# A fused state-space and expert kernel on one core: GpSimd's gate products spread over earlier slots, the skip factor folded into a weight

## The reference

```python
x = x + s6(layernorm(x))      # selective state space, 256 inner channels, 64 states
x = x + moe(layernorm(x))     # 8 experts, hidden size 256, top 2 of 8 weighted
x = x + s5(layernorm(x))      # diagonal complex state space, 64 states
x = x + moe(layernorm(x))     # the same experts again
```

```python
xs, res = split(x @ Wi + bi);  xs = silu(xs)
h = dA * h + dB * x_t                     # for each of 256 channels x 64 states
y_t = C_t * sum(h, axis=-1)
y = (y + xs * Dp) * silu(res)
z = y @ Wo + bo + residual                # then a layernorm with gamma, beta
```

## Time and profile before

| | |
|---|---|
| median of 3 runs | 1877.04 us (1875.87 to 1879.06) |
| the profiled execution | 1876.52 us, its span 1874.7 us |
| VectorE busy | 1523.8 us, 81% of the span |
| GpSimd busy | 1513.0 us, 81% |
| TensorE busy | 1333.3 us, 71% |
| ScalarE busy | 1291.4 us, 69% |
| mean granted TensorE clock | 0.861 of full speed |

### The profile page before, as it was taken

How to read it: one execution, slowest core, us unless ns; L and a number is a source line. 1 busy time by engine, 2 the same in 40 slices (tenths; PEclk the granted TensorE clock), 3 DMA queues, 4 the chain that set the end, 5 groups by cost and what they waited for, 6 DMA issues and landing times. The chain is left out here.

```text
span 1874.7 us, 19073 instructions
## 1 busy us (share of the span) xinstructions
PE 1333.3 (71%) x5928; PEld 601.0 (32%) x5928; DVE 1523.8 (81%) x2109; ACT 1291.4 (69%) x2285; POOL 1513.0 (81%) x888
## 2 busy tenths in 40 slices
PE   3236458778776877768776878668786777668958
PEld 1001123224332343324331343324332343324535
DVE  3988998888889788897899878988889878896322
ACT  4456668686787778777787778777787768765423
POOL 0899999978998699977998789986999789983312
PEclk8556569879997999979998899979999899979979
DMA  3511411122111310132111401132111221100000
GB/s 92 187 51 70 163 45 51 48 90 95 57 42 57 135 51 29 51 110 91 38 47 49 157 28 56 48 108 78 51 51 48 90 96 51 46 28 1 7 1 6
DMA packets 38749, 121.90 MB, mean 65 GB/s; under 512 B 5876, under 2 KB 21111, under 8 KB 26359
## 3 DMA queue, kind: packets, MB, share of 16 engines
q1 hardware_dynamic: 37062, 120.67, 18.1%
q10 hardware_dynamic: 1584, 0.01, 0.0%
HBM read 109.13 MB, written 11.53 MB: 64 GB/s over the span
## 5 line engine op out<-in xcount | busy, mean ns | idle before, releaser
L1180 DVE TENSOR_TENSOR_SCAN h<-da,w 128x512 f32<-128x512 f32 x1024 | 1191.0, 1207 | 148.9 <-ACT da L768 130.9
L878 POOL TENSOR_TENSOR w<-ur,br 128x1024 f32<-128x1024 f32 x512 | 1192.5, 2358 | 40.4 <-DVE h L1180 27.6
L768 ACT ACTIVATE da<-dr,al 128x511 f32<-128x511 f32 x1024 | 681.6, 687 | 219.5 <-DVE h L1180 216.5
L601 PE MATMUL ys<-h,wsum 128*32 128x512 f32 x2048 | 320.1, 702 | 222.2 <-DVE h L1180 202.8
L533 PE MATMUL bankH<-nT,w 128*128 128x512 f32 x512 | 309.3, 688 | 90.7 <-DVE aq L1118 86.3
L821 POOL TENSOR_TENSOR x<-x,yk 128x512 f32<-128x512 f32 x128 | 162.6, 1270 | 219.3 <-ACT yk L729 219.2
L547 PEld LDWEIGHTS bankY<-w,aq 128*128 128x128 f32 x2048 | 247.0, 192 | 85.4 <-issue 63.3
L533 PE MATMUL bankG<-nT,w 128*128 128x512 f32 x432 | 250.3, 663 | 24.6 <-DVE aq L1118 24.6
L547 PE MATMUL bankY<-w,aq 128*128 128x128 f32 x2048 | 254.3, 278 | 12.4 <-DVE aq L1118 7.9
L729 ACT ACTIVATE yk<-bankY,rt 128x128 f32<-128x128 f32 x512 | 151.2, 362 | 111.2 <-PE bankY L547 98.0
L601 PEld LDWEIGHTS ys<-h,wsum 128*32 128x32 f32 x2048 | 42.9, 114 | 422.2 <-DVE h L1180 388.0
(11 more groups left out here) (181 smaller groups left out, 1124.7 us busy)
## 6 DMA issues: line engine op xcount, KB each, us to landing
br<-b_rows SPq DMA_DIRECT2D x64, 1024.0 KB, 5.1
dr<-d_rows SPq DMA_DIRECT2D x16, 1024.0 KB, 6.9
ur<-u_rows SPq DMA_DIRECT2D x16, 1024.0 KB, 7.4
d_rows<-vh SPq DMA_DIRECT2D x16, 256.0 KB
u_rows<-th SPq DMA_DIRECT2D x16, 256.0 KB
xnew<-in_L_attn_a_x_dram SPq DMA_DIRECT2D x8, 256.0 KB, 5.2
w<-in_L_ffn_W_dram SPq DMA_DIRECT2D x2, 1024.0 KB, 11.1
x<-in_L_attn_a_x_dram SPq DMA_DIRECT2D x8, 256.0 KB, 9.0
```

Source lines behind the costliest of these rows:

```text
L601: ins = nc.tensor.matmul(ys[32 * q:32 * q + 32, :], wsum[:, :], h[:, (DUOS * t.b + 2 * group + q // 2) % H_RING, q % 2, :], start=(n == 0) ...
L768: A(da[duo % D_RING][:, k % 2, 1:L], dr[:, half, q, 1:L], ACT.Exp, scale=nega[:, QUADS * half + q, n:n + 1]).then_inc(decay_ready, 1)
L878: G.tensor_tensor(w[:, turn_duo % W_RING, :, :], ur[:, half, q:q + 2, :], br[:, chunk % B_RING, row:row + 1, :].to_broadcast([128, 2, L]), ...
L1180: V.tensor_tensor_scan(h[:, turn_duo % H_RING, k % 2, :], da[duo % D_RING][:, k % 2, :], w[:, turn_duo % W_RING, k % 2, :], 0.0, ALU.mult, ...
```

## The change

The products move to other slots and ScalarE's part of the skip term goes away. `cg` is now made in slots 30 and 36, `xd` in slots 33 and 39, `resa` in slot 42. `xd` is now xs * sres, without the factor Dp. Instead, ScalarE once multiplies the rows of Wo by Dp into a new tile `wod` (slot 40 of turn 0, two instructions of 128x128), and TensorE multiplies `xd` by `wod` in place of `wo`. The wait that keeps `xd` from being overwritten before z was computed moves from ScalarE to GpSimd.

```diff
-GATES_AT, RES_AT = 44, 54
+GATES_AT, SKIPS_AT, RES_AT, FOLD_AT = (30, 36), (33, 39), 42, 40
...
+                if known(c, 1):
+                    pe.wait_ge(skips_folded, 2)
                 pe.wait_ge(direct_ready, 2 * c + 2)
                 for a in range(TT):
                     for k in range(2):
-                        nc.tensor.matmul(p[:, a * 128:(a + 1) * 128], xd[:, k, a * 128:(a + 1) * 128], wo[:, k, :],
+                        nc.tensor.matmul(p[:, a * 128:(a + 1) * 128], xd[:, k, a * 128:(a + 1) * 128], wod[:, k, :],
...
-            def skips(t):
-
-                b = t.b
-                for half in range(2):
-                    yield GATES_AT + 3 * half
-                    if half == 0 and t.post:
-                        act.wait_ge(filled[BANK["z"]], t.before("z") + 1)
-                    A(xd[:, half, :], xs[:, half, :], ACT.Copy, scale=dps_[:, half:half + 1]).then_inc(skip_ready, 1)
+            def fold_skips():
+
+                yield FOLD_AT
+                act.wait_ge(late_loads, 16 * LATE_LOADS)
+                for k in range(2):
+                    A(wod[:, k, :], wo[:, k, :], ACT.Copy, scale=dps_[:, k:k + 1]).then_inc(skips_folded, 1)
...
-                weave(pair, [skips(t)] + tasks_of(t, pre_a, post, late))
+                weave(pair, ([fold_skips()] if known(t.b, 1) else []) + tasks_of(t, pre_a, post, late))
...
                 for half in range(2):
-                    yield GATES_AT + 3 + 3 * half
+                    yield GATES_AT[half]
...
                     G.tensor_tensor(cg[:, half, :], cm[:, half, :], sres[:, half, :], ALU.mult).then_inc(gate_ready, 1)
-                    yield GATES_AT + 4 + 3 * half
-                    pool.wait_ge(skip_ready, 2 * b + half + 1)
-                    G.tensor_tensor(xd[:, half, :], xd[:, half, :], sres[:, half, :], ALU.mult).then_inc(direct_ready, 1)
+                    yield SKIPS_AT[half]
+                    if half == 0 and t.post:
+                        pool.wait_ge(filled[BANK["z"]], t.before("z") + 1)
+                    G.tensor_tensor(xd[:, half, :], xs[:, half, :], sres[:, half, :], ALU.mult).then_inc(direct_ready, 1)
```

More of the change, by code:

```diff
@@ L227, in hybrid_kernel @@
         wi = sb("wi", [128, 2 * DI]); wx = sb("wx", [128, 2, 2 * NS + DI])
-        wdt = sb("wdt", [NS, DI]); wo = sb("wo", [128, 2, D]); wg = sb("wg", [128, E])
+        wdt = sb("wdt", [NS, DI]); wo = sb("wo", [128, 2, D]); wod = sb("wod", [128, 2, D]); wg = sb("wg", [128, E])
         w1 = sb("w1", [128, E, HID]); w2 = sb("w2", [128, E, HID]); w3 = sb("w3", [128, E, 2, D])
@@ L279, in hybrid_kernel @@
         scanned = sem("scanned"); summed = sem("summed"); ys_taken = sem("ys_taken")
-        gate_ready = sem("gate_ready"); skip_ready = sem("skip_ready"); direct_ready = sem("direct_ready"); c_ready = sem("c_ready"); res_ready = sem("res_ready")
+        gate_ready = sem("gate_ready"); skips_folded = sem("skips_folded"); direct_ready = sem("direct_ready"); c_ready = sem("c_ready"); res_ready = sem("res_ready")
         stats_ready = [sem(f"stats_ready{k}") for k in range(5)]; moments_ready = [sem(f"moments_ready{k}") for k in range(5)]
```

## The result

The change made the kernel slower by 0.2%: 1879.06 us (1877.43 to 1885.94, 20 runs) against 1876.24 us (1874.08 to 1880.69, 20 runs) of the kernel before, ratio 1.0019 [1.0011, 1.0027]. I had forecast 1864.6 us, with a range of 1855 to 1875. The profiled execution took 1878.37 us, its span 1876.5 us, at a mean granted clock of 0.853 (before 0.861).

What follows compares the result with a forecast made beforehand. The prediction took GpSimd's backlog to bound the stretch of slots 44 to 78. It summed 10.8 us (turns 1 to 6, 1.8 each) and 1.1 us (turn 7) to 11.9: 1876.5 - 11.9 = 1864.6 us, range 1855 to 1875.

Steps and rivals of the forecast that it cites:

- Slots 44 to 64: Scan of slot 52 0.8 us earlier, lost again at slot 54; slot 56 keeps 0.77, slot 60 a further 0.2.
- The layernorm: Slot 71: GpSimd's sum ends sooner, xn comes 1.83 us earlier, VectorE's stall goes and it is 1.7 us early.
- The last sum: Up to slot 78: GpSimd's last sum starts at 773.7, not 775.47; VectorE's statistics are 1.8 us early.
- Behind slot 78 all engines depend on each other alone, so I carry 1.8 us to the turn's end: Slot 78 to the turn's end: the 1.8 us are kept, 10.8 us over turns 1 to 6.
- The clock: At the turn's start TensorE's granted clock can give or take 1.4 us per turn; left open by the sum.
- the clock takes it back: Rival, 12%: earlier arrival at the turn's start meets a longer low stretch, 1.4 of each 1.8 us lost, 1873 us.
- turns stay at 215.0 us though the stalls went: Sign that the forecast is wrong: turns keep their length instead of being 1.8 us shorter.
- The cover of slots 30 to 44: GpSimd's five moved instructions, 6.1 us, fit into 6.7 us of idle time and lead; 0.6 left, cost 0.
- the lead runs out: Rival, 7%: the five instructions exceed the cover before slot 44, scans wait, 5 us slower, 1881.5 us.
- `nm` chain: Slot 71: ScalarE's 3.50 us wait for GpSimd's layernorm scale, costing VectorE 0.63 us; xn was to come 1.83 earlier.
- Turn 7: The last turn has no xn, so it gains only 1.1 us.
- ScalarE's part: Sixteen xd products, 11.3 us busy, go; freed time at slots 44 and 47 runs into a wait: 0, at most 8.5.

Runs made afterwards that it cites:

- the third filled pair: The kernels before and after, each with TensorE adding matmuls of zeros in most of its waits to hold its clock high: 1831.43 us and 1825.73 us.
- after_res54: The kernel after with only the residual's bias (resa) back in slot 54, no zeros added: 1879.34 us, ratio 1.0017.
- fold_only: The kernel after with GpSimd's five instructions back in slots 47 to 54, so only D is folded into a copy of Wo: 1880.87 us, ratio 1.002.
- the filled kernel after: The kernel after with TensorE adding matmuls of zeros in most of its waits, one of the third filled pair: 1825.73 us, ratio 0.9729.
- fill3_res54: The filled kernel after with only the residual's bias (resa) back in slot 54: 1819.72 us, ratio 0.9704.

## Why the prediction was wrong

The steps, by how far the scans of turn 3 are ahead of those of before, counted from slot 45 (the last row is slot 45 of turn 4, so it holds the cover of slots 30 to 44 as well). "Free" is after against before, "high" the third filled pair:

| slot | predicted | free | clock high |
|---|---|---|---|
| 52 | -0.8 | -0.80 | -0.81 |
| 54 | 0 | 0.00 | 0.00 |
| 56 | -0.77 | -0.77 | -0.80 |
| 64 | -0.97 | -1.00 | -1.03 |
| 71 | -1.7 | -0.17 | -1.77 |
| 78 | -1.8 | +0.74 | -1.88 |
| 100 | -1.8 | +2.58 | -1.87 |
| 109 | -1.8 | +1.31 | -1.88 |
| 4 | -1.8 | +0.11 | -1.88 |
| 45 | -1.8 | -0.01 | -0.67 |

*Slots 44 to 64* came out within 0.1 us: what moved, what was lost again at slot 54, and what slots 56 and 60 gave.

*The first step that failed* is the pair of terms "The layernorm" and "The last sum" (1.7 and 1.8). They took TensorE's tile times, and with them those of `yk` and the decays, from the rows of before. After, TensorE worked at 1.2 GHz in two stretches, behind slots 60 and 70, that did not exist before. The lead of 1.00 us at slot 64 is a lag of 0.54 at slot 65 and of 0.74 at slot 78, where I had 1.8 of lead: 2.5 us of a turn are gone here. With the clock high both terms are right.

*The second step that failed* is "Behind slot 78 all engines depend on each other alone, so I carry 1.8 us to the turn's end". With the clock free a difference is not carried. The kernel loses 1.1 us more by slot 88. TensorE comes back there from a wait of 5.69 us (5.84 before), and more of its work then meets the low clock: `stepsB`'s four records take 3.78 us (3.58 before) and the sums behind them 1.94 (1.07 before). So VectorE's wait for `bankY` behind slot 86, 1.39 us before, is

```profile
791.17 0.69 DVE L1142 TENSOR_TENSOR sq<-bankH,cosT 128x512 f32<-128x512 f32 x1 [2.32 <-PE bankY L577]
```

Another 0.7 us are lost by slot 100, since the step sizes of the next sequence (`bankH`, on whose result ScalarE waits) are made at the low clock too. Before and after, behind waits of one length:

```profile
803.43 1.12 PE L510 MATMUL bankH<-steps_and_b,wdt 64*128 64x512 f32 x2 [1.80 <-DVE sq L1157]
```

```profile
803.88 1.84 PE L510 MATMUL bankH<-steps_and_b,wdt 64*128 64x512 f32 x2 [1.80 <-DVE sq L1158]
```

Then the kernel gets 1.3 back at slot 109, where the low stretch now ends earlier among the router's tiles, and 1.2 at slot 4. The turn ends where it ended before. With the clock high the 1.88 us of turn 3 are carried to the end to the hundredth.

*The clock* I had weighed at the turn's start alone, at 1.4 us a turn. There it went my way (1.93 to 1.06 us in the earlier trace rows, turns 3 to 5), and it was the smallest part of the matter. The rival "the clock takes it back" had the right mechanism with a chance of 12% and the wrong amount, since it kept 0.4 us of each turn; the true figure for turns 3 to 6 is 0. In the profiled executions turns 0 and 1 were 1.8 us shorter in sum and turn 2 was 1.3 longer, after which both kernels repeat at the same length. The 1.8 us of the first turns are not to be trusted: `after_res54`, whose median is that of the kernel after, reaches turn 2 4.6 us later in its profiled execution. The even 215.0 us of two kernels' turns was in the rows, and I had listed "turns stay at 215.0 us though the stalls went" as what would prove me wrong. A length that settles after a transition and then repeats to 0.03 us needed an explanation before anything was subtracted from it.

The Trainium skill, page "TensorE: Matmul & The Clock Gate", section "HAM oscillation — how this bites in real kernels", says that a group behind a long stall, 3 to 5 us in its example, restarts at the low clock. The trace agrees behind the wait of 5.84 us (3.58 us for `stepsB`'s four records). The tiles at slot 61 show that near 3 us the length of the stall does not decide it: behind 2.94 us they ran at 2.4 GHz before the change, behind 2.74 us at 1.2 after it, and behind 2.96 us at 1.2 in `fold_only`.

*The cover of slots 30 to 44* held with the clock free, as forecast, with 0.4 us to spare (forecast 0.6). With the clock high it does not. The scans then come earlier, the lead of GpSimd's products is shorter, and the filled kernel after stands for products in slots 40 to 44. The view names no engine for these waits, but the products of slots 40 and 44 end 0.09 us before the scans start. Its VectorE there:

```profile
699.22 2.34 DVE L1198 TENSOR_TENSOR_SCAN h<-da,w 128x512 f32<-128x512 f32 x2 [0.59 <-issue]
...
706.31 2.34 DVE L1198 TENSOR_TENSOR_SCAN h<-da,w 128x512 f32<-128x512 f32 x2 [1.10 <-issue]
```

That is the 1.2 us between the last two rows of the table, my rival "the lead runs out". With `resa` left in slot 54 nothing is lost by slot 45, and the gain of 1.03 us up to slot 64 lasts a turn (-1.07), though the `nm` chain gives nothing more.

*Turn 7* (forecast -1.1) came out 1.7 us longer, at a granted clock of 0.80 from slot 56 to its last slot, where before it was 0.86. With the first scan 0.4 us later and the turns 0 to 2 together 0.5 shorter, that is 1.6 of the 1.85 us between the profiled executions; the rest, in the tail, and the later first scan stay open.

*ScalarE's part*, taken at 0, cannot be told from 0 with the clock high (1.5 us, with overlapping intervals), but it makes the scan of slot 52 0.45 us earlier, and with the clock free that is enough to move the tiles of slots 61 to 64 into a low stretch.

## What to carry to other kernels

Where a repeated stretch keeps one length to a few hundredths while its stalls move, find what holds it before counting a local saving as the total: lay TensorE's groups of the same shape beside each other and look for two durations a factor near two apart. If they are there, keep TensorE busy first (here zeros into an open accumulation, worth 2.4%), and tune the other engines afterwards, for the same edit that lost 0.2% then gained 0.3%, and 0.6% with one of its five instructions left in place. A test delay belongs behind the waits in question, and is to be run with the suspected cause present and removed.

## What the runs showed that I had not expected

- Raising the granted clock from 0.861 to 0.936 took 45 us off 1876, with TensorE busy for only 71% of the span before. The best kernel, `fill3_res54`, takes 1819.72 us, 3.0% less than before, though its zeros are 570 more records (285 matmuls) that keep TensorE busy for 274 us.
- A shift of 0.45 us by VectorE (`fold_only`) made a low stretch that cost 3.0 us by slot 66.
- Adding 1.2 us of work to each turn cost 0.0 in steady turns of 215.0 us, and 1.1 in turns of 207.1.
